# A four-layer transformer on one core: split tails moved to GpSimd, maxima issued by SyncE, planned waits of TensorE filled to their length

## What is computed

```
layer 0: full self-attention with mask and rotary embedding, masked cross-attention, gelu(tanh)
layer 1: full self-attention, cross-attention, gelu(tanh)
layer 2: self-attention in shifted windows of 128, cross-attention over the 16 largest scores, SwiGLU
layer 3: full self-attention and cross-attention, both with rotary embedding, gelu(erf)
x = x + gate * attention(norm(x)); x = x + gate * cross(norm(x), context); x = x + gate * mlp(norm(x))
```

## Time and profile before

| | us |
|---|---|
| median of 3 runs (2906.60 to 2916.17) | 2908.04 |
| the profiled execution | 2916.84 |
| its span, first to last instruction | 2915.0 |

### The profile page before, as it was taken

The page is one execution under the profiler, slowest core; times in us unless marked ns, Lnnn a source line. Parts: engine busy times, 40 slices in busy tenths (PEclk is TensorE's granted clock), DMA queues, the critical chain, the costliest instruction groups (busy, mean ns, idle before and its releaser), DMA issues. The chain is left out here.

```text
span 2915.0 us, 47676 instructions
## 1 busy us (share of the span) xinstructions
PE 2728.5 (94%) x15136; PEld 1351.8 (46%) x15136; DVE 1893.7 (65%) x4209; ACT 1425.8 (49%) x2579; POOL 590.3 (20%) x999
## 2 busy tenths in 40 slices
PE   8999999999989999999988888898999999999899
PEld 5444344335544424334455566656645323224456
DVE  5977388642574783866344889668974884885621
ACT  3455635574445583566644444333221674785441
POOL 2110001131331110331125323411020010112510
PEclk9999999999999999999998999999999999999899
DMA  6333122433452312233066516521420322123621
GB/s 207 69 104 107 41 72 71 112 89 98 144 172 53 114 51 67 91 115 95 22 186 186 167 50 195 146 85 60 147 60 1 116 60 52 45 61 108 183 92 38
DMA packets 268153, 286.78 MB, mean 98 GB/s; under 512 B 70665, under 2 KB 207243, under 8 KB 267275
## 3 DMA queue, kind: packets, MB, share of 16 engines
q1 hardware_dynamic: 256651, 282.28, 33.0%
q0 software_dynamic: 11264, 1.46, 0.3%
HBM read 167.43 MB, written 114.72 MB: 97 GB/s over the span
## 5 line engine op out<-in xcount | busy, mean ns | idle before, releaser
L1570 ACT ACTIVATE probs<-ring_b 128x512 f32<-128x512 f32 (+1 forms) x1728 | 921.8, 599 | 457.9 <-PE ring_b L1429 359.9
L1748 DVE TENSOR_REDUCE row_max<-ring_a 128x1 f32<-128x1024 f32 x512 | 602.0, 1218 | 151.7 <-PE ring_a L1385 150.9
L1429 PE MATMUL ring_b<-q_ring,k_ring 100*128 100x512 bf16 x1536 | 526.8, 381 | 10.5 <-ACT probs L1570 2.8
L1385 PE MATMUL ring_a<-k_ring,q_ring 96*128 96x512 bf16 x1536 | 450.1, 383 | 27.9 <-DVE row_max L1748 16.1
L1462 PE MATMUL ring_c<-probs,v_and_ones 128*17 128x512 f32 x3072 | 402.0, 599 | 1.8 <-ACT probs L1570 1.2
L1745 DVE CUSTOM_DVE_ANT_0 w_mlp<-ring_a,w_mlp 128x1024 bf16<-128x1024 f32 x256 | 302.1, 1222 | 49.6 <-PE ring_a L1385 48.4
L1868 POOL CAST neg_max_parts<-neg_max 16x128 bf16<-16x128 f32 x112 | 37.6, 336 | 1392.1 <-ACT neg_max L1564 1141.3
L1429 PEld LDWEIGHTS ring_b<-q_ring,k_ring 100*128 100x128 bf16 x1536 | 145.7, 97 | 349.9 <-issue 241.5
L1385 PEld LDWEIGHTS ring_a<-k_ring,q_ring 96*128 96x128 bf16 x1536 | 135.5, 98 | 250.5 <-issue 153.6
L1485 PE MATMUL ring_b<-h_feat,w_mlp 128*128 128x512 f32 x512 | 230.3, 595 | 1.4 <-ACT h_feat L1541 0.8
L1497 PE MATMUL ring_a<-w_mlp 128*128 128x256 f32 x1024 | 226.1, 380 | 5.0 <-DVE w_mlp L1803 2.4
(11 more groups left out here) (143 smaller groups left out, 3346.4 us busy)
## 6 DMA issues: line engine op xcount, KB each, us to landing
q_ring<-scr_q SPq DMA_DIRECT2D x128, 384.0 KB, 4.3
scr_q<-split SPq DMA_DIRECT2D x64, 384.0 KB, 2.6
k_ring<-scr_k SPq DMA_DIRECT2D x64, 384.0 KB, 5.0
scr_q<-split SPq DMA_DIRECT2D x64, 256.0 KB, 3.0
scr_out<-out_stage SPq DMA_DIRECT2D x128, 128.0 KB, 2.5
scr_out<-out_stage SPq DMA_DIRECT2D x64, 256.0 KB, 2.4
h_feat<-scr_out SPq DMA_DIRECT2D x56, 256.0 KB
reciprocals<-scr_recip SPq DMA_DIRECT2D x56, 256.0 KB
```

The costliest lines, as they stand in the source:

```text
L1385: last = mm(ps[:, half * BLOCK:(half + 1) * BLOCK], q[0:PARTS, h, t * P:(t + 1) * P], k_view(g)[0:PARTS, h, half * BLOCK:(half + 1) * BLOC ...
L1429: last = mm(ps[:, :], k_view(g)[0:ROWS, h, s.kt * P:(s.kt + 1) * P], q[0:ROWS, h, q0:q0 + BLOCK], start=not g.masked, stop=True)
L1570: f(PT[0:n, s.pt, :], ps[0:n, :], ACT.Exp, **kw).then_inc(b_evac, 1)
L1748: v.tensor_reduce(NM[:, s.nm, s.u:s.u + 1], ps, AX.X, ALU.max).then_inc(a_evac, 1)
```

## The change

Four things change. Steps of layer 3 that rotate and split (without the context keys) become two steps, `rotate` on TensorE and VectorE up to the first cast, and `tail` on GpSimd with the last three operations; whoever waited for the split waits for the tail's own semaphore. `max_put` goes from GpSimd's order to SyncE's. Fills take the whole planned wait, from 0.4 us on in both kinds. All ranks, `DELAY`, `REACH`, `LATER` and `SECOND` have new values, so every engine's order is another.

```
-            if rest > 0.8:
-                s["fill"] = int((rest - 0.3) * 0.7 / FILL_ONE)
+            if rest > 0.4:
+                s["fill"] = int(rest / FILL_ONE)
...
-            s["fill_o"], s["fill_on"], s["fill_ring"] = int((gap - 0.15) * 0.8 / FILL_ONE), self.count.get(o, 0), o
+            s["fill_o"], s["fill_on"], s["fill_ring"] = int(gap / FILL_ONE), self.count.get(o, 0), o
...
 RANK = dict(
...
-    cross_s=(6.3, -1.1, -4.2, 1.0),
-    mlp=(9.0, 8.0, 4.0, -1.4),
-    self_f=(-12, 18.8, -12, 11.8),
+    cross_s=(9.8, 4.8, 11.8, 9.8),
+    mlp=(10.7, 3.7, -0.3, 1.7),
+    self_f=(-9, 16.8, 7, 16.8),
...
-REACH = dict(PE=0.0, ACT=0.0, DVE=0.05, POOL=0.0, SP=0.2)
-DELAY = (7.5, 100)
+REACH = dict(PE=0.0, ACT=0.05, DVE=0.05, POOL=0.05, SP=0.0)
+DELAY = (7.5, 260)
...
-LATER = (-7, -6.5, -5, -40)
+LATER = (-13, -10.5, -36, -40)
 FILL_ONE = 0.11
+TAILS = (3,)
...
-        d = yield do("split", ([("PE", 0.264 if ck else 0.86)] if rope else []) + [("DVE", (2.08 if rope else 0.84) if ck else 4.3 if rope else 1.79)],
-                     after=[s], ring="a" if rope else None, counts=["split_n"], of=s, rope=rope, l=l)
+        if rope and l in TAILS and not ck:
+            t = yield do("rotate", [("PE", 0.86), ("DVE", 2.55)], after=[s], ring="a", counts=["turned_n"], of=s, l=l)
+            d = yield do("tail", [("POOL", 3.5)], after=[t], counts=["tail_n"], of=s, turned=t, l=l)
+        else:
+            d = yield do("split", ([("PE", 0.264 if ck else 0.86)] if rope else []) + [("DVE", (2.08 if rope else 0.84) if ck else 4.3 if rope else 1.79)],
+                         after=[s], ring="a" if rope else None, counts=["split_n"], of=s, rope=rope, l=l)
...
-        s = yield do("max_put", [("POOL", 2.15 if g.edge else 1.67)], after=[d], lat=2.6 if g.cross else 1.9, g=g, ms=ms, of=d)
+        s = yield do("max_put", [("SP", 1.4 if g.edge else 1.05)], after=[d], lat=2.2 if g.cross else 1.8, g=g, ms=ms, of=d)
...
+                elif s.kind == "max_put":
+                    g = s.g
+                    sp.wait_ge(max_split, s.of.msplit_n + 1)
+                    for j in range(3):
+                        sp.dma_start(QR[PARTS + 1 + j:PARTS + 2 + j, g.q, :], MS[:, s.ms, j, :]).then_inc(max_in[g.q], 16)
+                    if g.edge:
+                        sp.dma_start(QR[PARTS:PARTS + 1, g.q, :], KR[PARTS:PARTS + 1, 0, :]).then_inc(max_in[g.q], 16)
...
+                elif s.kind == "tail":
+                    f = s.of
+                    r = RAW[:, f.raw, 0:f.width]
+                    parts = SPLIT[:, f.split, :, 0:f.width]
+                    pool.wait_ge(turned, s.turned.turned_n + 1)
+                    link(g_.tensor_tensor(out=r, in0=r, in1=parts[:, 0, :], op=ALU.subtract))
+                    link(g_.tensor_copy(parts[:, 1, :], r))
+                    g_.tensor_tensor(out=parts[:, 2, :], in0=r, in1=parts[:, 1, :], op=ALU.subtract).then_inc(tail_done, 1)
```

More of the change, by code:

```diff
@@ L283 @@
 RANK = dict(
[L284 to L290, removed]
-    cross_s=(6.3, -1.1, -4.2, 1.0),
-    mlp=(9.0, 8.0, 4.0, -1.4),
-    self_f=(-12, 18.8, -12, 11.8),
[L294 to L299, removed]
-)
-REACH = dict(PE=0.0, ACT=0.0, DVE=0.05, POOL=0.0, SP=0.2)
-DELAY = (7.5, 100)
-SECOND = dict(init=-15, mod=-9, prep=-4, out=4, ctx=-24, load=-14, cross_f=7,
-              cross_s=13, mlp=-3, self_f=-3, self_pv=24, self_s=-8, tk=-5, tk_s=-20,
-              win_f=-19, win_s=4)
-LATER = (-7, -6.5, -5, -40)
+    init=(16.3, 4.9, 15.3, -0.1),
+    mod=(17.8, 17.8, 13.8, 14.8),
+    prep=(7.6, -5, -0.5, 21.8),
+    out=(2.0, -2, 7, -4),
+    ctx=(6.0, -4.0, 14.0, -3.0),
+    load=(-12, -9, -9, -9.2),
+    cross_f=(4.1, 7.4, -2.9, 7.8),
+    cross_s=(9.8, 4.8, 11.8, 9.8),
+    mlp=(10.7, 3.7, -0.3, 1.7),
+    self_f=(-9, 16.8, 7, 16.8),
+    self_pv=(13, 24, 13, 16),
+    self_s=(-5.8, 10.2, -1.8, 11.2),
+    tk=(13.2, 6.3, -9, -9),
+    tk_s=(6.8, 14.8, -5.3, 4.8),
+    win_f=(-6, -9, -12, -6.9),
+    win_s=(-0.2, -0.2, 8.8, 3.8),
+)
+REACH = dict(PE=0.0, ACT=0.05, DVE=0.05, POOL=0.05, SP=0.0)
+DELAY = (7.5, 260)
+SECOND = dict(init=5, mod=10, prep=-3, out=4, ctx=-3, load=-12, cross_f=-11,
+              cross_s=19, mlp=12, self_f=7, self_pv=17, self_s=-21, tk=12, tk_s=-5,
+              win_f=12, win_s=17)
+LATER = (-13, -10.5, -36, -40)
 FILL_ONE = 0.11
+TAILS = (3,)
 def rank_of(kind, l, b, blk):
@@ L996, in blocks_kernel, with split_ended @@
         xn_ready, ctxn_ready = sem("xn_ready"), sem("ctx_norm_ready")
-        split_done = sem("split_done")
+        split_done, turned, tail_done = sem("split_done"), sem("rotated"), sem("tail_done")
+        def split_ended(eng, d):
+            if d.kind == "tail":
+                eng.wait_ge(tail_done, d.tail_n + 1)
+            else:
+                eng.wait_ge(split_done, d.split_n + 1)
         scr_in = [sem(f"scratch_written_{i}") for i in range(SPLITS)]
@@ L1163, in _ @@
                     d, s = s.done, s.of
-                    sp.wait_ge(split_done, d.split_n + 1)
+                    split_ended(sp, d)
                     for j, parts in SCRATCH[s.which[-1]]:
@@ L1344, in _ @@
                     last.then_inc(b_full, 1)
-                elif s.kind == "split" and s.rope:
+                elif s.kind == "rotate" or s.kind == "split" and s.rope:
                     f = s.of
@@ L1676, in _ @@
                     v.tensor_tensor(GB[:, 0, :], ps[:, 0:FEAT], ROWS_IN[:, s.row.slot, :], ALU.add).then_inc(a_evac, 1)
-                elif s.kind == "split":
+                elif s.kind in ("split", "rotate"):
                     f = s.of
@@ L1680, in _ @@
                     parts = SPLIT[:, f.split, :, 0:f.width]
-                    if s.rope:
+                    if s.kind == "rotate" or s.rope:
                         dve.wait_ge(tables_in, 16 * 3)
@@ L1693, in _ @@
                         link(v.tensor_tensor(r, r, rot[:, 0:f.width], ALU.add))
-                        link(v.tensor_copy(parts[:, 0, :], r))
+                        if s.kind == "rotate":
+                            v.tensor_copy(parts[:, 0, :], r).then_inc(turned, 1)
+                        else:
+                            link(v.tensor_copy(parts[:, 0, :], r))
                     else:
                         dve.wait_ge(b_evac, f.bn + 1)
-                    link(v.tensor_tensor(r, r, parts[:, 0, :], ALU.subtract))
-                    link(v.tensor_copy(parts[:, 1, :], r))
-                    v.tensor_tensor(parts[:, 2, :], r, parts[:, 1, :], ALU.subtract).then_inc(split_done, 1)
+                    if s.kind == "split":
+                        link(v.tensor_tensor(r, r, parts[:, 0, :], ALU.subtract))
+                        link(v.tensor_copy(parts[:, 1, :], r))
+                        v.tensor_tensor(parts[:, 2, :], r, parts[:, 1, :], ALU.subtract).then_inc(split_done, 1)
                 elif s.kind in ("v", "ctx_v"):
@@ L1872, in _ @@
                     pool.wait_ge(max_split, s.msplit_n + 1)
-                elif s.kind == "max_put":
-                    g = s.g
-                    for j in range(3):
-                        pool.dma_start(QR[PARTS + 1 + j:PARTS + 2 + j, g.q, :], MS[:, s.ms, j, :]).then_inc(max_in[g.q], 16)
-                    if g.edge:
-                        pool.dma_start(QR[PARTS:PARTS + 1, g.q, :], KR[PARTS:PARTS + 1, 0, :]).then_inc(max_in[g.q], 16)
                 elif s.kind == "tk_shift":
```

6 lines of the change are left out of this document (3 added, 3 removed).

## The result

The changed kernel takes 2959.01 us, the median of 4 runs (2955.87 to 2963.30), against 2911.37 us for the kernel before in 4 runs (2906.60 to 2916.17): a ratio of **1.0165 (1.0139 to 1.0190)**, slower by 48 us (0.0165 x 2911). The prediction of 2866 us has the wrong sign, and its range, up to 2925, doesn't hold the time. The profiled execution has a span of 2961.5 us, 46.5 more than before.

A forecast was written before the change was run, and what follows sets the result against it. Bound: TensorE's fixed order with the waits in it. From the profiled 2916.8 us, +15 - 23 + 0 - 4 - 30 = -42 gives 2874.8, less 8.8 against the median: 2866 us; likeliest case 2835 to 2890, whole range 2825 to 2925.

The forecast's parts named there:

- Step 5: All engines' orders: new ranks and a later second batch lift stretches 1500 to 1600 and 2000 to 2100, -30 us.
- Step 2: TensorE's granted clock, 0.976: longer fills bring back half of 46 us of lost full clock, -23 us (0 to -46).
- the two worst stretches: 1500 to 1600 and 2700 to 2800 us: 24 us of the clock loss, held out of longer fills' reach.
- Step 1: TensorE's planned waits: 1120 more fills, which overrun where the plan is wrong, +15 us (0 to 46).
- Step 3: Copies of maxima issued by SyncE: less GpSimd issue against late landing and SyncE's in-order waits, 0 us (-12 to +30).
- Step 4: Layer 3's 24 split tails moved from VectorE to GpSimd: -4 us (-14 to +16).
- A: TensorE's 256 waits: full-length fills leave no slack, so delays stay until the end; slower, 2934 us, chance 0.17.
- B: Copies on SyncE: maxima delivered late, +30 us in place of 0, 2896 us, chance 0.15.
- C: Layer 3's tails on GpSimd and VectorE's operations hinder each other, +15 us in place of -4, 2885 us, chance 0.10.
- D: The new order brings no less waiting; only the clock and the tails count, 2896 us, chance 0.13.

The follow-up runs named there:

- the second experiment: The kernel before with fills to full length and from 0.4 us on, all orders the same: 2922.28 us, 1.0025.

## Why the prediction was wrong

**Step 5, the order, -30: the step that failed.** With its tails it measured +30, and 34 had been expected the other way. The bound was read from stretches: two stretches of layer 2 lifted to the level of a third. One was indeed lifted (2000 to 2100). But that an order lifts one stretch doesn't say that it keeps its neighbours, and 1600 to 1700 fell by 7 points. The forecast took "an order can gain this much" for "this order gains it", although no row favoured either sign; its own upper end on the slow side, +30, is what came. The wider distance between the batches, on which the -30 also rested, does nothing by itself (1.0004). Numbers were at hand that would have been better than rows of stretches: the plan's end, 2798.5 against 2808.7, a gain of 10 and not of 30, and the price on which it rests. The trace of before has SyncE issuing a copy of the same 4 KB, with each load of layer 0's cross-attention:

```profile
L1205 SPq DMA_DIRECT2D q_ring<-k_ring x16: 502/572/597, 493.5 to 856.4; - x16
```

Three of these are 1.7 us, where the changed planner says 1.05.

**Step 2, the clock, -23: mechanism right, size wrong.** The fills did raise the clock: by 0.010 on the kernel before, and from 0.968 to 0.978 on the changed one. What failed is the exchange rate. The forecast counted lost clock as lost time. Without fills 148 us of loss cost 25 us of time, so the 29 us regained in the second experiment are worth an estimated 5, or somewhat more, since that rate is a lower bound. The forecast also held that longer fills don't reach the two worst stretches, with their 25 and 34 fills; in the changed kernel these stretches hold 91 and 129, and the first rose from 0.86 to 0.94.

**Step 1, longer fills, +15: about right.** By step 2's rate the 7 us on the kernel before are an estimated 12 of overruns less 5 of clock; on the changed order 13 us plus some 5 make 18, or 7 with the copies on GpSimd. The upper end of 46 and the count of 2880 fills (2846 measured) held, and so did the reading of the earlier trace rows.

**Step 3, copies on SyncE, 0: too low.** 5 us with short fills, 16 with long ones, inside its range (-12 to +30). Of the two reasons named against it, the landing time isn't there; the place in an in-order queue is, with the transfers that stand behind the copies, which the forecast didn't name. The Trainium skill (DMA: Bandwidth & Descriptors, Specifications) gives about 1 us to the first byte on GpSimd's path and 0.6 on SyncE's; by it alone this part would save an estimated 6 us. The trace agrees only in part: the landing is 0.1 us shorter, the issue 0.1 us longer, and moving the copies back was faster.

**Step 4, tails, -4: right in sign on this order**, -12, and +11 with the ranks of before. The tail's length was overestimated (3.07 against 3.8 us).

**The rivals.** A, that long fills take the slack, was nearest with 2934 us and the only one with the right sign. Its mechanism is there (runs with nothing idle behind them doubled), but it is 2 to 13 of 48 us, and its 2934 needed 20 us of gain that didn't come. B, late maxima, is part of the 5 to 16 us of step 3, without its landing time. C, the port, is there in single operations, and the part still gained. D, an order that brings nothing, went the right way from -30 and stopped half way. The forecast was right that most of the gain would have to come from the order, and none of its rivals let the order be worse than nothing: that case had no chance of its own, although +30 stood in the bounds of the step.

**By its own tests**: over 2500 fills, yes. A clock of 0.985, no: 0.978. Waits for the copies: 31 us before and 29 after, or 33 and 36 with layer 0's fourth copy. Fills plus idle time should fall by 40 us and rose by 49. The forecast's "some 380 us" for it is another count than the 541 above: 194 of fills and the 187 us in which the earlier trace rows have no product running. By that one it went to 449 (313 and 136), up by 69.

## What to carry to other kernels

A planner's gain is worth no more than its prices: before trusting a new order, compare the plan's end with the chip for old and new, and measure each price that the change touches, because constants tuned under a price that is too low can lean on just that resource. Time lost to a lower clock isn't time lost at the end; one run without any fills gives a lower bound for the rate. An unsure term with bounds of both signs needs a rival that lives at its bad end, with a chance.

## What the runs showed of the hardware

Two engines held each other up in a place that the new order made. The timelines of GpSimd and of VectorE in the changed kernel:

```profile
2164.53 4.50 POOL L1867 TENSOR_TENSOR w_mlp<-w_mlp,gate 128x2048 f32<-128x2048 f32 x1 [1.52 <-DVE gate L1695]
...
2165.70 3.88 DVE L1816 TENSOR_TENSOR h_feat<-h_feat,reciprocals 128x512 f32<-128x512 f32 x1
```

A normalisation that takes 0.69 us in the median took 3.88 and ended at 2169.58, 0.55 us after GpSimd's long product at 2169.03; the longest took 5.00, beside another such product, and before the longest was 2.24, beside a product of 2.36 us. The forecast weighed a rule of the Trainium skill (SBUF - State Buffer, Who interferes with whom): a VectorE instruction with two inputs in SBUF contends with a GpSimd instruction that reads SBUF, and whoever has the shared ports keeps them for its whole instruction. These traces agree. The length that counts is GpSimd's, so it was the 4.5 us products of the gates, not the 1.2 us pieces of the tails, that cost most in one blow.

A DMA is issued in 0.484 us by GpSimd and in 0.589 us by SyncE for the same 4 KB, and lands in 2.0 and 1.9 us.
